# A macaron block on one core: the mixer's loop written out, and the feed-forward stages on six PSUM banks instead of eight

## The chip, the cores and the metric

The kernel runs on one core of one Trainium2 chip. The metric is device time in microseconds (us) of one execution of the whole program; three executions gave 3285.9, 3286.45 and 3291.64 us, median 3286.45. Engines are named as in the profile: PE (TensorE matmul), PEld (its weight loads), DVE (VectorE), ACT (ScalarE), POOL (GpSimd), SP (the engine that issues most transfers). Differences below 0.2% (6.6 us) are taken as no change.

## The reference

The input is 8 sequences of 1024 tokens with 256 channels, fp32. Three stages follow each other:

```python
x = x + 0.5 * ffn(layernorm(x), w_gate, w_up, w_down)
x = x + mixer(layernorm(x), ...)            # Mamba-like selective scan
x = x + 0.5 * ffn(layernorm(x), w_gate, w_up, w_down)

def ffn(x, ...):                            # every linear layer on fp4-rounded operands
    gate = fp4_linear(x, w_gate)            # 256 -> 704
    y = fp4_linear(x, w_up)                 # 256 -> 704
    return fp4_linear(silu(gate) * y, w_down)   # 704 -> 256

def mixer(h, ...):                          # 256 -> 2 x 512, conv over 4 tokens, silu
    x, z = split(h @ in_proj_w)
    x = silu(causal_conv(x))
    dt_r, B, C = split(x @ x_proj_w)        # 64, 16, 16 columns
    delta = softplus(dt_r @ dt_proj_w + b)
    # for each of 512 channels and 16 states, over 1024 tokens:
    #   s = exp(delta * A) * s + delta * B * x ;  y = sum over states of C * s
    return ((y + x * D) * silu(z)) @ out_proj_w
```

`fp4_linear` rounds both operands in blocks of 16 to a grid of 4-bit values before multiplying in fp32.

## The kernel before

**Stages.** The program runs `ffn` (with the preparation of the weights in front), `mixer`, `ffn`. Each of the three is a block of its own; all engines meet between blocks. Results between the stages lie in DRAM.

**Feed-forward.** `ffn` works on T = 32 tiles of 256 tokens, as two halves t = 0, 1 of 128 tokens. It is software-pipelined by hand: in step j each engine works on tiles j+4 to j-4 at once. The order on each engine is written in its `step` function; semaphore counts order the engines against each other. `span` (L22) writes the first eight steps and the last out as straight code and puts 16 steps, as two rounds of eight, into a hardware loop (`Fori`). PE in one step, before: `gate_up(0)` first part, `turn_h(0)`, `gate_up(0)` second part, `down(0)`, `gate_up(1)` first part, `turn_h(1)`, `gate_up(1)` second part, `turn_x`, `down(1)`. Here `gate_up` (L700) multiplies 256 channels by 1408 columns into `psG` (three banks), `turn_h` (L718) transposes the 704 hidden channels of tile j-2 into `psH` (two banks, 768 of 1024 columns used), `turn_x` (L727) transposes the quantised input of tile j+1 into `psX` (one bank), and `down` (L735) multiplies by the down weights into `psD`, one bank for each half. That makes eight banks. ACT copies `psH` to `hT` (L637, L638) and `psX` to `xT` (L677); DVE reads `psD` in `result` (L488). Semaphores `hT_kept`, `xT_kept`, `y_done` and `x_turned` tell that these were done.

**Mixer.** It runs round by round, one batch a round (`program(r, R, full)`), for r = -1 to 8: round r scans batch r and prepares parts of batches r+1 and r-1. A round has 64 slots; in each, DVE does one multiplication (L1129) and one scan (L1117) over 1024 tokens for 128 pairs of channel and state, POOL one multiplication (L962), ACT one exponential (L1063), and PE the replication of `du` (L1230), part of the sum over states (L1212), and the small jobs of a table (`JOBS`: projections, convolution, output) through two banks. The function `rounds` (L855) sets which rounds are straight code: r = -1, 0, then a hardware loop that runs three times over two rounds (r = 1 to 6), then r = 7, 8. In the loop, semaphore targets and addresses come from registers.

## Time and profile before

| what | value |
|---|---|
| median of three executions | 3286.45 us |
| profiled execution | 3285.56 us, of it span 3283.5 us |
| first feed-forward stage with preparation | to about 645 us of the span |
| mixer, from first to last scan | 751.5 to 2657 us |
| second feed-forward stage | from about 2690 us to the end |
| PE, DVE, POOL, ACT busy over the span | 83%, 81%, 66%, 52% |
| mean granted PE clock | 0.889 of full speed |

The time outside the span is 3285.56 - 3283.5 = 2.1 us. A share of the whole span is a mean over three stages with different limits, so the stages are read one by one, by stretches of the timeline. PE's records overlap their neighbours a little, so that a PE that is 50.00 of 50 us busy is one that never waits, not one at its peak.

### The profile page before, as it was taken

Reading aid. Unit: us, or ns where it says so; the run is one execution under the profiler, and the core shown is the slowest. Engines: PE = TensorE matmul, PEld = TensorE weight load, DVE = VectorE, ACT = ScalarE, POOL = GpSimd, SP = SyncE. Lnnn points to the kernel's source line nnn. Section 1 sums busy time; section 2 is a strip of 40 time slices with the busy share of each in tenths; the row PEclk is TensorE's granted clock in tenths of the full one; section 3 lists DMA queues with packets and bytes.
Section 4 is the critical chain, followed back from the end, with each engine's and each line's share of the span. In section 5 each row is a group of like instructions: output and inputs, shape, how many; then the busy total and the mean of one; then the engine's idle time right before and its main releaser. Section 6 shows DMA issues by size and latency. Waiting matters only on the chain. (4 is left out here: it accounts for less than half of the span.)

```text
span 3283.5 us, 33864 instructions
## 1 busy us (share of the span) xinstructions
PE 2736.3 (83%) x10349; PEld 1403.1 (43%) x10349; DVE 2652.0 (81%) x2498; ACT 1695.5 (52%) x2363; POOL 2174.0 (66%) x1219
## 2 busy tenths in 40 slices
PE   3999999776878978868878868978867659999998
PEld 1565656453324424414414414424412125555565
DVE  6777777408999999989999989999999946777774
ACT  3444444335756656656665655666654513444442
POOL 4566665306887877767778777777787735555552
PEclk9999999887978979969978968979966679999999
DMA  3011111108687676776777766776767720111000
GB/s 102 20 49 42 46 48 39 51 11 204 145 192 177 165 190 171 172 186 158 175 186 175 181 163 171 180 180 167 183 170 184 187 78 13 33 33 32 26 26 20
DMA packets 173331, 388.08 MB, mean 118 GB/s; under 512 B 22502, under 2 KB 90150, under 8 KB 172902
## 3 DMA queue, kind: packets, MB, share of 16 engines
q1 hardware_dynamic: 155382, 367.06, 45.0%
q10 hardware_dynamic: 17776, 18.94, 1.9%
q8 instruction: 81, 1.33, 0.2%
q14 instruction: 92, 0.75, 0.1%
HBM read 308.26 MB, written 52.49 MB: 110 GB/s over the span
## 5 line engine op out<-in xcount | busy, mean ns | idle before, releaser
L962 POOL TENSOR_TENSOR mix_scan<-mix_scan,mix_bc 128x1024 f32<-128x1024 f32 x512 | 1204.5, 2355 | 423.0 <-DVE mix_scan L1117 422.7
L1117 DVE TENSOR_TENSOR_SCAN mix_scan<-mix_decay,mix_ps_du 128x1024 f32<-128x1024 f32 x512 | 1170.0, 2285 | 72.8 <-ACT mix_decay L1063 23.5
L1129 DVE TENSOR_TENSOR mix_ps_du<-mix_ps_du,mix_bc 128x1024 f32<-128x1024 f32 x512 | 618.5, 1208 | 148.2 <-PE mix_ps_du L1230 142.3
L1230 PE MATMUL mix_ps_du<-mix_stack,mix_sel 96*128 96x512 bf16 x1024 | 367.9, 447 | 394.2 <-DVE mix_scan L1117 360.9
L711 PE MATMUL ffn_ps_gate_up<-ffn_w_gate_up,ffn_xT 128*128 128x512 f32 (+1 forms) x1536 | 662.3, 568 | 14.6 <-DVE ffn_h L479 13.0
L1063 ACT ACTIVATE mix_decay<-mix_decay,mix_a_neg 128x1024 f32<-128x1024 f32 x512 | 573.5, 1141 | 116.1 <-DMA mix_decay<-delta_rows 115.2
L741 PE MATMUL ffn_ps_down<-ffn_w_down,ffn_hT 128*128 128x256 f32 (+1 forms) x1536 | 386.4, 394 | 12.4 <-ACT ffn_hT L638 12.4
L711 PEld LDWEIGHTS ffn_ps_gate_up<-ffn_w_gate_up,ffn_xT 128*128 128x128 f32 x1536 | 273.4, 191 | 281.4 <-issue 231.2
L1230 PEld LDWEIGHTS mix_ps_du<-mix_stack,mix_sel 96*128 96x128 bf16 x1024 | 78.9, 103 | 707.3 <-DVE mix_scan L1117 581.6
L1212 PE MATMUL mix_ps_y<-mix_scan,mix_red 128*32 128x512 f32 x2048 | 342.1, 750 | 5.4 <-POOL mix_scan L962 5.4
L479 DVE TENSOR_TENSOR ffn_h<-ffn_silu_gate,ffn_ps_gate_up 128x704 f32<-128x704 f32 x128 | 113.6, 887 | 279.1 <-ACT ffn_silu_gate L643 279.1
L611 POOL TENSOR_TENSOR ffn_h_scaled<-ffn_h,ffn_h_recip 128x1408 f32<-128x1408 f32 x64 | 188.4, 2944 | 225.2 <-ACT ffn_h_recip L683 225.2
L741 PEld LDWEIGHTS ffn_ps_down<-ffn_w_down,ffn_hT 128*128 128x128 f32 (+1 forms) x1536 | 276.2, 191 | 107.7 <-issue 56.5
L637 ACT ACTIVATE ffn_hT<-ffn_ps_turned 128x640 f32<-128x640 f32 x128 | 89.9, 703 | 316.0 <-PE ffn_ps_turned L723 316.0
L1169 PE MATMUL mix_ps_job<-mix_xin,mix_conv_diag 128*128 128x256 f32 x1024 | 247.6, 386 | 2.3 <-ACT mix_xin L1015 2.3
L1169 PEld LDWEIGHTS mix_ps_job<-mix_xin,mix_conv_diag 128*128 128x128 f32 x1024 | 191.3, 191 | 86.7 <-issue 50.4
L605 POOL TENSOR_TENSOR ffn_hq<-ffn_h_scaled,ffn_h_scale 128x1408 f32<-128x1408 f32 x64 | 165.7, 2590 | 70.1 <-DVE ffn_h_scaled L534 65.9
L1021 ACT ACTIVATE mix_u<-mix_ps_job,mix_conv_b 128x256 f32<-128x256 f32 x128 | 60.2, 470 | 223.7 <-PE mix_ps_job L1169 223.7
L591 POOL TENSOR_TENSOR ffn_mv<-ffn_mv,ffn_eps 128x2 f32<-128x2 f32 x64 | 33.0, 516 | 210.0 <-DVE ffn_mv L516 205.5
L1190 PE MATMUL mix_ps_job<-mix_hnT,mix_w_in 128*128 128x512 f32 x256 | 157.1, 746 | 8.0 <-ACT mix_hnT L1000 6.6
L1162 PE MATMUL mix_ps_job<-mix_hnT,mix_w_in 128*128 128x256 f32 x512 | 145.8, 437 | 5.3 <-ACT mix_hnT L1000 5.3
L969 POOL TENSOR_TENSOR mix_delta<-mix_delta,mix_delta_u 128x1024 f32<-128x1024 f32 x32 | 75.4, 2355 | 105.8 <-ACT mix_delta_u L1080 105.8
(133 smaller groups left out, 3638.5 us busy)
## 6 DMA issues: line engine op xcount, KB each, us to landing
mix_decay<-delta_rows SPq DMA_DIRECT2D x512, 512.0 KB, 6.8
mix_stack<-mix_parts SPq DMA_DIRECT2D x384, 64.0 KB, 2.0
delta_rows<-mix_delta SPq DMA_DIRECT2D x32, 512.0 KB, 3.1
ffn_x<-_attn_hidden_states_dram SPq DMA_DIRECT2D x32, 256.0 KB, 2.9
after_ffn<-ffn_y SPq DMA_DIRECT2D x32, 256.0 KB, 3.0
normed_ffn<-ffn_y_normed SPq DMA_DIRECT2D x32, 256.0 KB, 3.0
mix_x_tokens<-normed_ffn SPq DMA_DIRECT2D x32, 256.0 KB, 11.8
mix_x_residual<-after_ffn ACTq DMA_DIRECT2D x32, 256.0 KB, 2.9
```

The lines of the kernel that those rows point to most:

```text
L605: G.tensor_tensor(blocks(hq[:, l2, :]), blocks(hn[:, l2, :]), spread(hs[:, (j - 1) % 4, :]), ALU.mult).then_inc(sig.hq_done, 1)
L611: G.tensor_tensor(blocks(hn[:, j % 2, :]), blocks(h[:, j % 2, :]), spread(hr[:, :]), ALU.mult).then_inc(sig.hn_done, 1)
L711: ins = M(psG[:, lo:hi], xT[:, j % 2, (t * KX + k) * P:(t * KX + k + 1) * P], wgu[:, k, lo:hi], start=(k == 0), stop=(k == KX - 1))
L741: ins = M(psD[:, t, 0:D], hT[0:c, t, k * P:(k + 1) * P], wd[0:c, k, :], start=(k == 0), stop=(k == KH - 1))
L962: G.tensor_tensor(wt, wt, bc[:, r % 2, 1, :], ALU.mult).then_inc(hc_done, 1)
L1063: A.activation(da[:, at % SPREADS, :], da[:, at % SPREADS, :], ACT.Exp, scale=const.aneg[:, qi:qi + 1]).then_inc(exp_done, 1)
L1117: V.tensor_tensor_scan(w[:, slot % RING, :], da[:, slot % SPREADS, :], ps_du[:, slot % 2, :], 0.0, ALU.mult, ALU.add).then_inc(scan_done, 1)
L1129: V.tensor_tensor(ps_du[:, slot % 2, :], ps_du[:, slot % 2, :], bc[:, r % 2, 0, :], ALU.mult)\
L1169: ins = M(job[:, 0:QT], const.conv_diag[:, c, t, :], xin[:, c, t:t + QT], start=(t == 0), stop=(t == TAPS - 1))
L1190: ins = M(job, const.w_in[:, k, DI + c * P:DI + (c + 1) * P], hnT[:, par, k, h * 512:(h + 1) * 512], start=(k == 0), stop=(k == KD - 1))
L1212: ins = M(y[32 * q:32 * q + 32, :], const.red[:, i, :, :].rearrange("p a b -> p (a b)"), w[:, (4 * m + q) % RING, h * 512:(h + 1) * 512], ...
L1230: ins = M(ps_du[:, slot % 2, h * 512:(h + 1) * 512], const.sel[0:SEL, i, :], stack[:, c % 2, q, h * 512:(h + 1) * 512], start=True, stop=True)
```

## The change

There are two parts. In the mixer, `rounds` writes all ten rounds out as straight code. In the feed-forward, `psX` and the second bank of `psD` go: `psD` and the first half of the transposed x share one bank, and the second half of x takes the spare columns of `psH`. `turn_x` is split into `turn_x(0)`, now ahead of `turn_h(1)`, and `turn_x(1)`, now behind `down(1)`; ACT's copy is split into two copies `keep_x(0)` (ahead of `keep_h(1)`) and `keep_x(1)` (behind `silu(1)`). Since an engine must not read a bank while PE writes into it, waits are added: `down(0)` waits for `result(1)` of the step before, `turn_x(0)` and `down(1)` for `result(0)`, `down(1)` for `keep_x(0)`, `turn_h(0)` for `keep_x(1)`. The two banks that come free are not used by anything else.

```diff
-    psH = ps_turned[:, :, :].rearrange("p a b -> p (a b)")
-    psX = a.ps("x_turned", [P, 512])
-    psD = a.ps("down", [P, 2, 512])
+    psT = ps_turned[:, :, :].rearrange("p a b -> p (a b)")
+    psDX = a.ps("down", [P, 2, D])
+    psH, psD = psT[:, 0:KH * P], psDX[:, 0, :]
+    psX = [psDX[:, 1, :], psT[:, KH * P:KH * P + D]]
...
+        def keep_x(t, j, i):
+            act.wait_ge(sig.x_turned, i * 2 + (t + 3))
+            if t == 0 and on(j, i, -1):
+                act.wait_ge(sig.gate_up_done, i * 2)
+            A.activation(xT[:, (j + 1) % 2, t * D:(t + 1) * D], psX[t], ACT.Copy).then_inc(sig.xT_kept, 1)
...
-                if t == 0:
-                    pe.wait_ge(sig.xT_kept, i + 1)
+                pe.wait_ge(sig.xT_kept, i * 2 + (t + 1))
...
+            if t == 0 and on(j, i, 0):
+                pe.wait_ge(sig.xT_kept, i * 2 + 2)
...
-        def turn_x(j, i):
-            pe.wait_ge(sig.xq_done, i + 2)
-            if on(j, i, 0):
-                pe.wait_ge(sig.xT_kept, i + 1)
-            for n in range(2 * KX):
-                ins = nc.tensor.transpose(psX[:, n * P:(n + 1) * P], xq[:, (j + 1) % 2, n * P:(n + 1) * P], ident[:, :])
+        def turn_x(t, j, i):
+            if t == 0:
+                pe.wait_ge(sig.xq_done, i + 2)
+                if on(j, i, -2):
+                    pe.wait_ge(sig.y_done, i * 2 - 3)
+            elif on(j, i, -2):
+                pe.wait_ge(sig.hT_kept, i * 2 - 2)
+            for k in range(KX):
+                n = t * KX + k
+                ins = nc.tensor.transpose(psX[t][:, k * P:(k + 1) * P], xq[:, (j + 1) % 2, n * P:(n + 1) * P],
+                                          ident[:, :])
...
-            if on(j, i, -3):
-                pe.wait_ge(sig.y_done, i * 2 + (t - 5))
+            if on(j, i, -3) or (t == 1 and on(j, i, -2)):
+                pe.wait_ge(sig.y_done, i * 2 + (t - 4))
+            if t == 1 and on(j, i, 1):
+                pe.wait_ge(sig.xT_kept, i * 2 + 3)
...
-            pairs = (B - 2) // 2
-            for r in range(-1, 1):
-                program(r, r, False)
-            if pairs > 0:
-                with eng.Fori(0, pairs) as it:
-                    for k in range(2):
-                        program(1 + k, it * 2 + (1 + k), True)
-            for r in range(1 + 2 * pairs, B + 1):
+            for r in range(-1, B + 1):
                 program(r, r, False)
```

In PE's order, one step of the feed-forward loop stands before as follows (`ffn_ps_down` is `psD`, `ffn_ps_turned` is `psH`; a wait on a row with REGISTER_ALU stands ahead of that register operation):

```order
L711 MATMUL ffn_ps_gate_up<-ffn_w_gate_up,ffn_xT 128x384 x2
L736 REGISTER_ALU
L738 REGISTER_ALU [waits ffn_hT_kept]
L741 MATMUL ffn_ps_down<-ffn_w_down,ffn_hT 128x256 [waits ffn_y_done]
...
L711 MATMUL ffn_ps_gate_up<-ffn_w_gate_up,ffn_xT 128x384 x2
L728 REGISTER_ALU
L732 MATMUL ffn_ps_x_turned<-ident,ffn_xq 128x128 [waits ffn_xT_kept,ffn_xq_done]
L732 MATMUL ffn_ps_x_turned<-ident,ffn_xq 128x128 x3
L736 REGISTER_ALU
L741 MATMUL ffn_ps_down<-ffn_w_down,ffn_hT 128x256 [waits ffn_y_done,ffn_hT_kept]
L741 MATMUL ffn_ps_down<-ffn_w_down,ffn_hT 128x256 x5
```

And the same step now:

```order
L748 REGISTER_ALU
L755 MATMUL ffn_ps_down<-ffn_w_down,ffn_hT 128x256 [waits ffn_y_done,ffn_hT_kept]
...
L743 MATMUL ffn_ps_down<-ident,ffn_xq 128x128 [waits ffn_y_done,ffn_xq_done]
...
L716 MATMUL ffn_ps_gate_up<-ffn_w_gate_up,ffn_xT 128x384 x2
L748 REGISTER_ALU
L752 REGISTER_ALU [waits ffn_y_done,ffn_hT_kept]
L755 MATMUL ffn_ps_down<-ffn_w_down,ffn_hT 128x256 [waits ffn_xT_kept]
L755 MATMUL ffn_ps_down<-ffn_w_down,ffn_hT 128x256 x5
L743 MATMUL ffn_ps_turned<-ident,ffn_xq 128x128 [waits ffn_hT_kept]
```

The first matmul of `down(0)` no longer has a register operation between its wait for `hT_kept` and itself; that of `down(1)` now has one, and it follows `gate_up(1)` directly, with no transposes of x between.

On DVE at the end of a round in the mixer (the scans stand under the name SCALAR_TENSOR_TENSOR), before (the end of the loop's body, and then what follows it):

```order
L1126 REGISTER_ALU
L1129 TENSOR_TENSOR mix_ps_du<-mix_ps_du,mix_bc 128x1024 [waits mix_rep_du]
L1117 SCALAR_TENSOR_TENSOR mix_scan<-mix_decay,mix_ps_du 128x1024 [waits mix_y_made,mix_dbu_done,mix_exp_done]
L862 REGISTER_ALU
L862 COMPARE_AND_BRANCH
L1129 TENSOR_TENSOR mix_ps_du<-mix_ps_du,mix_bc 128x1024 [waits mix_taken_B,mix_rep_du]
```

And the end of the same round now:

```order
L1138 TENSOR_TENSOR mix_ps_du<-mix_ps_du,mix_bc 128x1024 [waits mix_rep_du]
L1126 SCALAR_TENSOR_TENSOR mix_scan<-mix_decay,mix_ps_du 128x1024 [waits mix_y_made,mix_dbu_done,mix_exp_done]
L1138 TENSOR_TENSOR mix_ps_du<-mix_ps_du,mix_bc 128x1024 [waits mix_rep_du]
L1126 SCALAR_TENSOR_TENSOR mix_scan<-mix_decay,mix_ps_du 128x1024 [waits mix_y_made,mix_dbu_done,mix_exp_done]
L1138 TENSOR_TENSOR mix_ps_du<-mix_ps_du,mix_bc 128x1024 [waits mix_taken_B,mix_rep_du]
L1126 SCALAR_TENSOR_TENSOR mix_scan<-mix_decay,mix_ps_du 128x1024 [waits mix_y_made,mix_dbu_done,mix_exp_done]
```

The branch and the register operations of the loop are gone from DVE's list; the multiplications and scans stand as they did.

## Rows read from the trace of the kernel before

**Rows 1.** Page, part 2: busy tenths in 40 slices.

```profile
PE   3999999776878978868878868978867659999998
DVE  6777777408999999989999989999999946777774
```

**Rows 2.** Stretches: start:end, length, busy (x) PE PEld DVE ACT POOL, PEclk, DMA, GB/s.

```profile
300.00:350.00 50.00, 50.00 (x189) 30.17 (x188) 37.39 (x68) 23.91 (x45) 33.05 (x31) 1.00 0.15 48
```

**Rows 3.** Stretches between first scans: round 0; rounds 1-6; round 2; round 3.

```profile
751.46:984.16 232.70, 176.68 (x676) 74.04 (x675) 221.67 (x131) 148.00 (x172) 184.12 (x80) 0.84 0.76 182
984.16:2428.03 1443.87, 1181.45 (x4657) 542.95 (x4656) 1339.15 (x792) 895.10 (x1050) 1111.23 (x481) 0.85 0.72 175
1224.39:1469.77 245.38, 198.11 (x779) 90.78 (x778) 223.33 (x132) 149.26 (x176) 186.32 (x81) 0.85 0.73 178
1469.77:1705.55 235.78, 193.60 (x775) 89.39 (x774) 222.91 (x132) 149.03 (x175) 184.13 (x80) 0.86 0.71 172
```

**Rows 4.** Timeline, the loop's two jumps back: start, us, instruction, [idle before <-releaser].

```profile
1460.00 2.29 DVE L1117 TENSOR_TENSOR_SCAN mix_scan<-mix_decay,mix_ps_du 128x1024 f32<-128x1024 f32 x1
1465.59 1.89 PE L1230 MATMUL mix_ps_du<-mix_stack,mix_sel 96*128 96x512 bf16 x4 [6.03 <-issue]
1468.34 1.23 DVE L1129 TENSOR_TENSOR mix_ps_du<-mix_ps_du,mix_bc 128x1024 f32<-128x1024 f32 x1 [6.06 <-PE mix_ps_du L1230]
...
1949.33 1.23 DVE L1129 TENSOR_TENSOR mix_ps_du<-mix_ps_du,mix_bc 128x1024 f32<-128x1024 f32 x1 [5.79 <-issue]
```

**Rows 5.** DMA queues in 1460 to 1470 us: kind, packets, MB, share.

```profile
q14 instruction: 4, 0.03, 1.3%
```

**Rows 6.** DVE's waits in rounds 1 to 6: us, times, longest.

```profile
DVE mix_ps_du L1129 <- PE mix_ps_du L1230: 33.7, 24, 6.1
DVE mix_scan L1117 <- DVE mix_ps_du L1129: 11.6, 61, 0.2
DVE mix_scan L1117 <- issue: 2.7, 6, 0.5
```

**Rows 7.** Timeline of DVE in straight code, round 0.

```profile
783.05 2.29 DVE L1117 TENSOR_TENSOR_SCAN mix_scan<-mix_decay,mix_ps_du 128x1024 f32<-128x1024 f32 x1
785.26 1.21 DVE L1129 TENSOR_TENSOR mix_ps_du<-mix_ps_du,mix_bc 128x1024 f32<-128x1024 f32 x1
786.55 2.29 DVE L1117 TENSOR_TENSOR_SCAN mix_scan<-mix_decay,mix_ps_du 128x1024 f32<-128x1024 f32 x1
```

**Rows 8.** Stretches ahead of slot 51, rounds 2 and 3.

```profile
1408.00:1414.00 6.00, 6.00 (x14) 1.14 (x13) 5.76 (x5) 4.50 (x6) 3.84 (x2) 0.50 1.07 232
1651.00:1657.00 6.00, 5.34 (x20) 1.58 (x20) 5.82 (x4) 5.09 (x7) 4.38 (x2) 1.00 1.03 245
```

**Rows 9.** Timeline, single matmuls on PE in the first feed-forward stage.

```profile
306.19 0.70 PE L711 MATMUL ffn_ps_gate_up<-ffn_w_gate_up,ffn_xT 128*128 128x512 f32 x1
307.58 0.59 PE L711 MATMUL ffn_ps_gate_up<-ffn_w_gate_up,ffn_xT 128*128 128x512 f32 x1
311.68 0.45 PE L741 MATMUL ffn_ps_down<-ffn_w_down,ffn_hT 128*128 128x256 f32 x1
612.55 0.38 PE L741 MATMUL ffn_ps_down<-ffn_w_down,ffn_hT 128*128 128x256 f32 x1
615.43 0.33 PE L723 MATMUL ffn_ps_turned<-ident,ffn_hq 128*128 128x128 f32 x1
```

**Rows 10.** Timeline of one feed-forward step, 301 to 319 us.

```profile
301.86 0.70 ACT L637 ACTIVATE ffn_hT<-ffn_ps_turned 128x640 f32<-128x640 f32 x1 [4.22 <-PE ffn_ps_turned L723]
302.87 0.60 PE L732 MATMUL ffn_ps_x_turned<-ident,ffn_xq 128*128 128x128 f32 x4
303.73 0.59 ACT L677 ACTIVATE ffn_xT<-ffn_ps_x_turned 128x512 f32<-128x512 f32 x1
316.32 0.41 DVE L488 SCALAR_TENSOR_TENSOR ffn_y<-ffn_ps_down,ffn_x 128x256 f32<-128x256 f32 x1
318.16 0.82 PE L723 MATMUL ffn_ps_turned<-ident,ffn_hq 128*128 128x128 f32 x6
```

More of the change, by code:

```diff
@@ L487, in result @@
                     dve.wait_ge(sig.yn_done, i - 5)
-            V.scalar_tensor_tensor(y[:, (j - 2) % 4, t, :], psD[:, t, 0:D], 0.5, x[:, (j - 2) % 8, t, :],
+            V.scalar_tensor_tensor(y[:, (j - 2) % 4, t, :], psD, 0.5, x[:, (j - 2) % 8, t, :],
                                    ALU.mult, ALU.add).then_inc(sig.y_done, 1)
@@ L523, in step @@
                 if on(j, i, -1):
-                    dve.wait_ge(sig.x_turned, i)
+                    dve.wait_ge(sig.x_turned, i * 2)
                 V.tensor_tensor(blocks(xq[:, (j + 1) % 2, :]), blocks(xt[:, :]), spread(xs[:, (j + 1) % 2, :]),
@@ L668, in step @@
                 ins.then_inc(sig.xn_done, 1)
+            if on(j, i, 1):
+                keep_x(0, j, i)
             if on(j, i, -2):
@@ L673, in step @@
             if on(j, i, 1):
-                act.wait_ge(sig.x_turned, i + 2)
-                if on(j, i, -1):
-                    act.wait_ge(sig.gate_up_done, i * 2)
-                A.activation(xT[:, (j + 1) % 2, :], psX[:, :], ACT.Copy).then_inc(sig.xT_kept, 1)
+                keep_x(1, j, i)
             if on(j, i, 2):
@@ L736, in down @@
             pe.wait_ge(sig.hT_kept, i * 2 + (t - 3))
-            if on(j, i, -3):
-                pe.wait_ge(sig.y_done, i * 2 + (t - 5))
+            if on(j, i, -3) or (t == 1 and on(j, i, -2)):
+                pe.wait_ge(sig.y_done, i * 2 + (t - 4))
+            if t == 1 and on(j, i, 1):
+                pe.wait_ge(sig.xT_kept, i * 2 + 3)
             for k in range(KH):
                 c = min(P, F - k * P)
-                ins = M(psD[:, t, 0:D], hT[0:c, t, k * P:(k + 1) * P], wd[0:c, k, :],
+                ins = M(psD, hT[0:c, t, k * P:(k + 1) * P], wd[0:c, k, :],
                         start=(k == 0), stop=(k == KH - 1))
@@ L748, in step @@
                     gate_up(t, j, i, 0)
+                if t == 1 and on(j, i, 1):
+                    turn_x(0, j, i)
                 if on(j, i, -2):
@@ L752, in step @@
                     gate_up(t, j, i, 1)
-                if t == 1 and on(j, i, 1):
-                    turn_x(j, i)
                 if on(j, i, -2):
                     down(t, j, i)
+                if t == 1 and on(j, i, 1):
+                    turn_x(1, j, i)
         span(pe, step, -1, T + 2, 8, base)
```

## The prediction

> **What bounds the kernel now.** I read the busy tenths first, to cut the span into stages, and find three [rows 1]: slices 2 to 8 and 34 to 39, where PE stands at 9, and the long middle, where DVE does. A stretch of the feed-forward then shows PE busy 50.00 of 50 us, with DVE at 37.39 and ACT at 23.91 [rows 2]. So in the feed-forward every nanosecond that is added to PE's queue counts, and one added elsewhere counts only once it makes PE wait. In the mixer the stretches from a round's first scan to the next one's show DVE busy 221.67 of 232.70 us in round 0, and 1339.15 of 1443.87 us in the six rounds of the loop [rows 3]. DVE's idle time is what can be won there: 11.0 us in round 0, 104.7 us in rounds 1 to 6, thus 17.5 us for each. Scans follow each other at 3.50 us in straight code (783.05 to 786.55), which is 2.29 + 1.21, so nothing but idle time can go [rows 7].
>
> **The mixer's loop, the jump back.** A loop that runs three times jumps back twice. At the first jump the scan starts at 1460.00 and ends at 1462.29, and the next multiplication starts at 1468.34: DVE is idle for 6.06 us. PE, which is to give it the replicated row, itself sat for 6.03 us for nothing that the profile shows ("issue"), and DVE's second jump costs 5.79 us [rows 4]. In those 10 us the queue that carries instructions moved four packets of 8 KB (0.03 MB) [rows 5]. Round 2, which ends in such a jump, takes 245.38 us, and round 3, which does not, 235.78 [rows 3]. I take the jump as a refetch of code, all engines at once. Straight code has no jump, and rounds 0 and 7 run as straight code already. Gain 6.06 + 5.79 = 11.9 us, all on the engine that bounds the stage.
> What the Trainium skill says of it goes both ways. "Advanced Engine Details and Errata", section "Control Flow Timing", gives about 108 ns for a compare-and-branch; by that alone the two jumps would be worth 0.2 us, and I would have 11.7 us less to promise. "Runtime: NRT & Kernel Launch", section "Instruction fetch mechanics", says that a taken branch whose target lies outside the fetched window stalls for a transfer. The trace agrees with the second: 6.06 us.
>
> **The mixer's loop, register operations.** Inside the loop, 61 scans start late by 11.6 us in all behind the multiplication, 0.19 us each, and 6 more by 2.7 us for "issue" [rows 6]. In straight code the gap between multiplication and scan is 786.55 - 785.26 - 1.21 = 0.08 us [rows 7]. What goes with the registers is 11.6 - 61 x 0.08 = 6.7 us and 2.7 - 6 x 0.08 = 2.2 us, 8.9 us together. Bounds: nothing, if the gap has another cause than the register operation ahead of it, and 104.7 - 6 x 11.0 - 11.9 = 26.8 us, if the six rounds came to idle as little as round 0. The upper end is too high, since round 0 has no output jobs of an earlier batch. I take the 8.9 that has rows of its own.
> What stays: DVE's other waits for the replicated row, 33.7 - 11.9 = 21.8 us over six rounds [rows 6]. Part of them hangs on PE's clock. Ahead of slot 51 the granted clock is 0.50 in round 2 (1.2 GHz) and 1.00 in round 3 (2.4 GHz) [rows 8], and in the first DVE then waits some 2 us. Rounds begin some 6 us earlier from round 3 on, so such moments fall elsewhere: I keep the sum and put 5 us to either side. Mixer: -11.9 - 8.9 = -20.8 us.
>
> **The feed-forward, PE's own time.** The number of matmuls and transposes does not change; their neighbours do.
> First, `down` ends on a tile of 64 rows, and the weight load behind it is not hidden: the first matmul of `gate_up` lasts 0.70 us instead of 0.59. Transposes behind `down` occur in the drain of the stage, where the first lasts 0.33 us [rows 9], against 0.27 for an undisturbed one: six last 0.82 and four 0.60, so 0.11 for each start, and 0.60 - 3 x 0.11 = 0.27 [rows 10]. With `turn_x(1)` behind `down(1)`, 0.11 us is replaced by 0.06: -0.05 us in each of 29 steps that have both, in two stages, -2.9 us.
> Second, the first matmul of `down(0)` lasts 0.45 us in the loop and 0.38 outside [rows 9]: there a register operation stands between its wait for `hT_kept` and itself. By the new order `down(0)` loses this operation and `down(1)` gains it, and loses the cover of the transposes of x (0.44 us from start to start, 302.87 to 303.31). I count +0.07 and -0.07 for the 16 loop steps; if only one of the two happened, it would be 16 x 2 x 0.07 = 2.2 us to either side.
> Third, in the first two steps of each stage PE waits for the chain of silu and product, and `turn_x` lay in that wait. Now `turn_x(0)` stands in the chain, two transposes of 0.11 us in 2 steps of 2 stages: +0.9 us.
> Feed-forward: -2.9 + 0 + 0.9 = -2.0 us.
>
> **The feed-forward, the new waits.** Each was placed on the step from 301 to 319 us [rows 10].
> `turn_x(0)` waits for `result(0)`: that ends at 316.32 + 0.41 = 316.73, and the transposes would start where `turn_h(1)` does now, at 318.16. Slack 1.4 us; queued behind are `turn_h(1)`, `gate_up(1)` and with them silu and DVE.
> `down(1)` waits for the same and for `keep_x(0)`. ACT copies 640 columns in 0.70 and 512 in 0.59 us, hence 256 in about 0.37. It is idle for 4.22 us before `keep_h(1)`, and the copy runs while PE does the six transposes of `turn_h(1)`, 0.65 us. ACT is free again some 0.3 us before `keep_h(1)` may start. This is the narrowest place: `hT_kept` has no slack towards `down(1)`.
> `turn_h(0)` waits for `keep_x(1)`, which follows `down(1)` by 0.22 us of transposes and 0.4 us of copying, and has the 3.4 us of `gate_up(0)` to do it. `down(0)` waits for `result(1)` of the step before, whose bank is free some 3 us ahead.
> Behind `keep_x(1)` on ACT stand the small rescalings of the reciprocals, which wait for DVE until about then. Cost of all these waits: nothing, by these slacks; if one fails, it is paid 58 times.
>
> **The sum.** 3285.56 us of the profiled execution (3283.5 of span and 2.1 around it) - 20.8 - 2.0 = 3262.8. The median stands 0.9 us above the profiled execution, so 3263.7, rounded 3264 us, 0.7% less.
>
> **Rivals.**
> (a) Only the jumps go. The gaps of 0.19 us stay or come back as waits for PE at its lower clock, and the feed-forward gives nothing: 3286.5 - 11.9 = 3274.5 us, up to 3279 with 5 us of clock against it. For it: DVE still has 21.8 us of waits for PE that an earlier DVE only lengthens. Against it: DVE, not PE, ends nearly every slot. 0.15.
> (b) No change. The straight code has to be fetched as well, and a fetch under a loaded DMA (0.71 to 0.76 busy, rows 3) stalls the sequencers as often as the jump did: 3283 us. Against it: round 0 is straight code, under the same load, with the least idle time. Under this I also count the 0.1 us jump, whose sum is 3286.5 - 0.2 - 8.9 - 2.0 = 3275 us, with 0.01 of the chance. 0.07.
> (c) Slower. `keep_x(0)` reaches ACT late, so `keep_h(1)` starts after it and PE waits in front of `down(1)` in every step. From 22.8 / 58 = 0.4 us of wait in each step the gain is gone. If ACT gets to `keep_x(0)` only where it now gets to L637 (301.86), the wait is 0.37 us plus two hand-overs of about 0.1, 0.6 us: 58 x 0.6 = 35 us, 3263.7 + 35 = 3299 us. For it: no slack at this place, and PE bound. Against it: the 4.22 us of idle time of ACT. 0.08.
> (d) More than forecast, the loop's rounds coming near to round 0's idle time: 26.8 us in place of 8.9 at most, half of it -9 us, 3255 us. 0.08.
>
> **How the numbers follow.** The forecast has 0.62, with a range of its own from 3257 to 3271 (clock 5 us, feed-forward 2.2 us). The range for 8 in 10 takes in (d) and most of (a): 3255 to 3280 us; (c) and half of (b) lie outside. A measurement of this kernel tells 0.2% (6.6 us) from no change. Faster by more: the forecast, (a), (d) and the 0.01 of (b), together 0.85 (0.62 + 0.15 + 0.08), less 0.02 for clocks against (a), 0.83. Within 0.2%: (b) and this remainder, 0.08. Slower: (c) and a weaker form of it, 0.09.
>
> **What the profile after would show.** No idle time of 6 us on DVE between the last scan of rounds 2 and 4 and the next multiplication, and both rounds near 239 us. The group of waits of DVE's scan for its own multiplication gone from DVE's list. In the feed-forward PE still at 50.00 of 50 us, the first matmul of `gate_up(0)` at 0.59 us, and the transposes behind `down(1)` starting with 0.33. The forecast is wrong if rounds 1 to 6 take more than 1443.87 - 15 us together, if a step of the feed-forward gets longer than now by 0.1 us or more, or if PE's waits name `psX`'s new readers, L488 or ACT's copy of x.

## The result, and the profile after

The changed kernel takes 3249.02 us in the median (3248.44 to 3251.86, 4 runs), against 3287.19 us (3285.9 to 3291.64, 4 runs) of the kernel before in the same measurement: ratio 0.9883, 95% interval 0.9866 to 0.99. That is 38 us less, where 23 were forecast, and lies outside the range of 3255 to 3280. The sign and both mechanisms of the forecast hold; a third one, PE's clock, which it had set down as "5 us to either side", makes up most of the difference.

Two words are used throughout. A slot is measured on DVE, from the start of one scan to the start of the next; 3.5 us is a slot without a stall. Silu is ACT's silu in the feed-forward; there are two in each step, and a step's length is from one to the next but one. Every row and every slot length is from one profiled execution of its kernel, and executions of one kernel differ by several microseconds, so where that execution lies far from the median the text says so.

The page, part 2, shows the same three stages as in [rows 1]:

```profile
PE   2999999776878878978978978878867659999998
DVE  6777777407999999999999999999999946777775
```

From stage to stage, by the start of the first and last silu and scan in both traces:

| stretch | before | after | difference |
|---|---|---|---|
| start to first scan (feed-forward 1) | 751.5 | 750.4 | -1.1 |
| round 0 | 232.7 | 232.7 | 0.0 |
| rounds 1 to 6 | 1443.9 | 1414.0 | -29.9 |
| round 7, to its last scan | 227.1 | 227.5 | +0.4 |
| last scan to first silu of feed-forward 2 | 59.8 | 58.8 | -1.0 |
| from its first to its last silu | 536.5 | 535.5 | -1.0 |
| from there to the end | 32.0 | 27.6 | -4.4 |

The stretches of the mixer, which answer to [rows 3] (columns as in [rows 2]): rounds 1 to 6, and round 3. In the first DVE is busy almost as long as before (1337.64 against 1339.15 us), so 28.3 of the 29.9 us were its idle time.

```profile
983.17:2397.19 1414.02, 1170.33 (x4657) 540.01 (x4656) 1337.64 (x793) 894.38 (x1050) 1111.44 (x481) 0.86 0.73 179
1451.50:1687.30 235.80, 194.27 (x777) 89.59 (x776) 222.86 (x132) 149.10 (x175) 185.19 (x81) 0.86 0.74 179
```

At the place of the first jump [rows 4], DVE's timeline now has one scan 3.50 us after the other, with nothing idle between:

```profile
1447.96 2.29 DVE L1126 TENSOR_TENSOR_SCAN mix_scan<-mix_decay,mix_ps_du 128x1024 f32<-128x1024 f32 x1
1450.17 1.21 DVE L1138 TENSOR_TENSOR mix_ps_du<-mix_ps_du,mix_bc 128x1024 f32<-128x1024 f32 x1
1451.46 2.29 DVE L1126 TENSOR_TENSOR_SCAN mix_scan<-mix_decay,mix_ps_du 128x1024 f32<-128x1024 f32 x1
```

Of DVE's waits in rounds 1 to 6 (us, times, longest) the group of the scan behind its own multiplication, 61 times in [rows 6], is gone. The wait for the replicated row fell by 8.4 us from the 33.7 of [rows 6]. 6.1 of them are the first jump. The second, 5.8 us, was a group of its own in the kernel before; its row comes first, those of the changed kernel behind it:

```profile
DVE mix_ps_du L1129 <- issue: 5.8, 1, 5.8
```
```profile
DVE mix_ps_du L1138 <- PE mix_ps_du L1239: 25.3, 18, 2.6
DVE mix_scan L1126 <- ACT mix_decay L1072: 15.5, 17, 1.6
DVE mix_u L1147 <- PE mix_ps_y L1225: 3.2, 6, 0.8
DVE mix_scan L1126 <- issue: 0.9, 2, 0.5
```

The lengths of the slots, summed over rounds 1 to 6, say where the 29.9 us are: slot 63 (jumps) -12.6, slot 51 -9.4, slot 35 -2.3, slot 15 +3.2, the other 60 slots -8.7, of which 8.0 went in the gap between multiplication and scan. Slot 51 lasts 7.5 to 7.7 us in rounds 1, 2, 4 and 5 before and 4.5 in the other two; now it is long in round 5 alone. Slots 48 to 50 show how, in round 4 and in round 5 (here and below the last three columns are granted clock, DMA, GB/s):

```profile
1865.74:1876.24 10.50, 9.91 (x31) 2.98 (x30) 10.23 (x7) 7.72 (x12) 7.06 (x4) 1.00 1.04 231
2101.54:2112.37 10.83, 10.70 (x27) 3.22 (x25) 10.36 (x6) 7.21 (x10) 7.12 (x4) 0.66 0.98 223
```

The work is the same, the clock 1.00 and 0.66: the replicated row for slot 51 comes in time in the one and late in the other. In round 5 PE had been thinly busy ahead of this, 6.18 of 10.50 us in slots 44 to 46; in slot 47 it is at 0.50, the lower of its two levels (1.2 GHz). But PE was as thinly busy in round 4, 6.18 us in the same three slots, and its clock fell there too, to 0.68 in slot 47 (the first row below); it was back at 1.00 in slot 48. So a lower clock follows the thin work in both rounds, and what differs is how low it goes and how long it stays. Slot 15 is long (7.3 us) in all six rounds now, where it was 6.2 to 7.4 before, with the same pattern; PE is busy 3.38 of 7.00 us in slots 12 and 13, and in slots 14 and 15 the clock is 0.64:

```profile
1862.24:1865.74 3.50, 3.50 (x15) 1.44 (x15) 3.41 (x3) 0.55 (x1) 2.36 (x2) 0.68 1.02 226
...
2087.54:2098.04 10.50, 6.18 (x32) 2.86 (x34) 10.23 (x6) 7.28 (x9) 7.08 (x4) 0.93 1.03 237
2098.04:2101.54 3.50, 3.50 (x12) 1.32 (x13) 3.41 (x2) 0.56 (x1) 2.35 (x2) 0.50 1.05 240
...
1730.29:1737.29 7.00, 3.38 (x18) 1.64 (x20) 6.82 (x4) 5.47 (x8) 4.70 (x3) 0.82 1.02 237
1737.29:1748.12 10.83, 10.83 (x37) 5.02 (x30) 6.93 (x4) 5.36 (x7) 5.90 (x3) 0.64 1.04 242
```

In the feed-forward PE is still busy 50.00 of 50 us, as in [rows 2]. The first matmul of `gate_up(0)` now lasts 0.59 us and the transposes behind `down(1)` start with 0.33, as forecast from [rows 9]:

```profile
300.00:350.00 50.00, 50.00 (x189) 29.97 (x188) 37.63 (x71) 24.41 (x48) 33.01 (x32) 1.00 0.15 48
```
```profile
305.38 0.33 PE L743 MATMUL ffn_ps_turned<-ident,ffn_xq 128*128 128x128 f32 x1
...
305.65 0.59 PE L716 MATMUL ffn_ps_gate_up<-ffn_w_gate_up,ffn_xT 128*128 128x512 f32 x1
```

### The profile page after: what moved, and what is told of

Read it like the earlier page. It is cut to its first block and busy times, and to the rows that moved or that the text cites. A ratio compares the mean times of both kernels' runs of the same rounds, so it can differ in the third digit from the quotient of the medians.

```text
span 3246.6 us, 31734 instructions
## 1 busy us (share of the span) xinstructions
PE 2717.0 (84%) x10349; PEld 1394.6 (43%) x10349; DVE 2650.3 (82%) x2498; ACT 1705.8 (53%) x2427; POOL 2175.2 (67%) x1219
## 5 line engine op out<-in xcount | busy, mean ns | idle before, releaser
L646 ACT ACTIVATE ffn_xT<-ffn_ps_down 128x256 f32<-128x256 f32 x64 | 24.6, 384 | 230.4 <-PE ffn_ps_down L743 230.4
```

## The experiments

Medians of the kernel before, on the same chip as each group of runs: 3285.31 us for the first four, 3283.83 for the next four, 3284.19, 3285.38 and 3285.53 for those after. A "long slot 51" is one of 7.3 us or more. Two theories stood against each other throughout: REGISTERS, that register operations and jumps make the stalls by themselves, and CLOCK, that they only move a round against the moments at which PE runs at half its clock.

**One part at a time.** `e1_unroll_only` has only the mixer's part of the diff, `e2_ffn_only` only the feed-forward's.

> Only the mixer's rounds are written out; the feed-forward is that of the kernel before. Both theories give 3287 less 30 (rounds 1 to 6 were 29.9 us shorter together in the changed kernel): 3255 to 3260 us, if the mixer's part does all of it by itself. Theory CLOCK (of the 29.9 us, 21 are the jumps and the register gaps on DVE; 9 are stalls of 3 us ahead of slot 51 that fall away in three of four rounds because PE's clock happens to be high there): the number of rounds with a 7.5 us slot 51 may differ from the changed kernel's one, so 3255 to 3267. Theory REGISTERS (the 9 us are register operations on PE and ACT ahead of slot 51): at most one such round, 3255 to 3260.

> Only the feed-forward's part (six banks, x in halves); the mixer keeps its loop. From the trace of the changed kernel a step takes 17.19 us in place of 17.24 in the loop and 17.12 in place of 17.16 outside, 1.0 to 1.4 us a stage, so 3284 to 3285 us from the terms alone. CLOCK: a shift of the mixer by about 1 us may move the stalls ahead of slot 51 too, so up to 6 us to either side, and the number of 7.5 us slots 51 (4 in the kernel before) changes. REGISTERS: still 4 such slots, 3284 to 3285 us.

Measured: 3255.26 us (3253.6 to 3262.22; ratio 0.9899 to 0.993) and 3283.04 (3279.4 to 3286.37, 11 runs; 0.9982 to 1.0). The straight code gives 30 of the 38 us, and rounds 1 to 6 take 1414.0 us in it, as in the changed kernel. The feed-forward alone gives 2.3 us, and its interval reaches up to no change; that the steps are shorter is read from the traces further down. e2 has four long slots 51 like the kernel before, but in rounds 1, 2, 3 and 6 and not in 1, 2, 4 and 5.

**Jump against register operations.** `e3_one_pass` puts rounds 1 to 6 into a loop of one pass, `e4_one_jump` rounds 1 to 4 into a loop of two, `e5_regs_no_jump` rounds 1 to 5 into a loop with a step of 2 that is entered once; `e6_hint` is the kernel before with a prefetch hint for the loop's head.

```diff
# e3
+            with eng.Fori(0, 1) as it:
+                for k in range(6):
+                    program(1 + k, it * 6 + (1 + k), True)
# e4
+            with eng.Fori(0, 2) as it:
+                for k in range(2):
+                    program(1 + k, it * 2 + (1 + k), True)
# e5
+            with eng.Fori(0, 2, 2) as it:
+                for k in range(5):
+                    program(1 + k, it + (1 + k), True)
# e6
-                with eng.Fori(0, pairs) as it:
+                with eng.bass.Fori(0, pairs, engines=bass.OrderedEngineSet([eng.engine]), hint_back_edge=True) as it:
```

> The kernel before, but the loop runs once over six rounds: every wait still takes its target from a register, and no jump back is taken. If a jump costs 6 us and nothing else changes: 3287 - 12 = 3275 us, and the 0.19 us gaps between multiplication and scan are still there. REGISTERS: the stalls ahead of slot 51 stay in all or most of rounds 1 to 6, 3275 to 3280 us. CLOCK: the stalls may fall to one or two rounds with all register operations in place, then 3266 to 3272 us.

> The kernel before, but the loop runs twice over rounds 1 to 4, and rounds 5 and 6 are straight code. One jump of 6 us is left, 6 us fall away, and a third of the 9 us of register gaps: 3287 - 6 - 3 = 3278 us. The jump stands between rounds 2 and 3 with DVE idle for about 6 us; none between 4 and 5. REGISTERS: slot 51 stalls in rounds 1, 2 and perhaps 4, never in 5 and 6. CLOCK: no such pattern, total 3272 to 3281 us.

> The kernel before, but rounds 1 to 5 stand in a loop that runs once (it counts 0, then 2, up to 2), so that targets and addresses still come from registers and no jump back is taken; round 6 is straight. Theory CLOCK (stalls of 3 us ahead of slot 51 depend on where PE's clock falls, and not on register operations): 3285 - 12 for the jumps, the 0.19 us gaps stay in five rounds, and the stalls in slot 51 are as rare as in straight code if rounds of 235 us keep the clock's pattern: 3260 to 3266 us. Theory REGISTERS (the operations themselves bring the stalls): 4 or 5 of 5 rounds with a 7.5 us slot 51, 3270 to 3275 us.

> The kernel before with its loop of three passes, but each engine gets a prefetch hint for its jump back at the head of the loop. If the 6 us at a jump are the refetch of code (as the prediction has it), the idle time of DVE at 1462 and 1943 us shrinks from 6 us to under 1 us, total 3285 - 11 = 3274 us or less, down to 3262 if the stalls ahead of slot 51 go too. If the 6 us are something else of the loop (the register operations, the compare itself), nothing changes: 3285 us.

Measured: e3 3252.09 us (3251.32 to 3255.78), but its trace has none of the 0.19 us gaps and no 6 us of idle time: the loop of one pass had come out as straight code, so it tells nothing of register operations. Its one long slot 51 is in round 2, though, and not in round 5 as in e1 and the changed kernel. e4 3276.47 (3272.23 to 3280.61, 10 runs; the profiled one is the fastest), one jump of 6.2 us and long slots 51 in rounds 1, 2 and 3. e5 3273.67 (3272.47 to 3275.75): no jump, so the jumps are worth about 10 us, but 18 us above straight code, with 0.19 us gaps and a long slot 51 in every round from 1 to 6. e6 3268.65 (3265.27 to 3272.51): the 6 us at the jump are gone although it is taken twice, with 0.20 us left on DVE there, so they were the fetching of code:

```profile
1459.28 1.21 DVE L1129 TENSOR_TENSOR mix_ps_du<-mix_ps_du,mix_bc 128x1024 f32<-128x1024 f32 x1
1460.68 2.29 DVE L1117 TENSOR_TENSOR_SCAN mix_scan<-mix_decay,mix_ps_du 128x1024 f32<-128x1024 f32 x1 [0.20 <-DVE mix_ps_du L1129]
```

So far REGISTERS looked well: their gaps are 5 to 6 us, and the kernel pays 18 with them. But in e5 the straight round 6 had its slot 51 long too.

**Shifting straight code.** In `e7_shift1` and `e8_shift3` DVE writes a spare tile (896 columns) once, or three times, in round 1 of the changed kernel, and nothing else differs.

```diff
+                    if r == 1 and slot in (0,):        # e8: (0, 2, 4)
+                        V.memset(pause[:, :], 0.0)
```

> The changed kernel with one write of 896 columns (about 0.5 to 1 us) on DVE ahead of slot 0 of round 1, used by nothing: it shifts everything behind it. CLOCK: the pattern of granted clocks falls elsewhere, 1 to 5 of the rounds 1 to 6 have a 7.5 us slot 51, total 3250 to 3262 us. REGISTERS or a fixed structure: just the pause, 3250 us, with one such round as before.

> As the last, but with three such writes (ahead of slots 0, 2 and 4 of round 1), about 2 to 3 us. CLOCK: again another pattern, 3251 to 3263 us, and the number of 7.5 us slots 51 differs between the two shifted kernels. REGISTERS or a fixed structure: 3251 to 3252 us, one such round.

Measured: 3251.79 us (3249.66 to 3257.78) and 3257.91 (3253.1 to 3260.03). The profiled execution of e8, a typical one, has a long slot 51 in rounds 1, 2 and 5. That of e7 has them in rounds 1 and 2, but it is the slowest of four by 5 us and differs already in round 0, ahead of the added write (slot 51 lasts 6.5 us there), so its pattern can't be put down to the write. So slots 51 get long in straight code too, and in other rounds after a shift (e8) or without one (e3, e7). Over the profiled executions up to here they were long in 20 of 27 rounds with register operations and in 9 of 33 straight ones of rounds 1 to 6: a bias, no rule.

**Whose registers.** `e11_regs_pe` and `e12_regs_dve` are e5 with the register operations on one engine; all others have straight code.

```diff
+            looped = eng.engine == nc.tensor.engine     # e12: nc.vector.engine
+            for r in range(-1, 1 if looped else B + 1):
+                program(r, r, False)
+            if looped:
+                with eng.Fori(0, 2, 2) as it:
+                    for k in range(5):
+                        program(1 + k, it + (1 + k), True)
+                for r in range(6, B + 1):
+                    program(r, r, False)
```

> The kernel before with the rounds straight on every engine but PE; on PE rounds 1 to 5 keep their register operations (a loop that runs once, so without a jump). With them on all engines it was 3273.67, with them on none 3255.26. PE'S REGISTERS (they delay the replicate matmuls and with them move the clock): slot 51 long in three rounds or more, 3264 to 3270, while the 0.19 us gaps ahead of the scans are gone. DVE'S REGISTERS: 3252 to 3258, slot 51 long in one round or so.

> The same with the register operations on DVE alone. DVE'S REGISTERS (each delayed scan lengthens its slot, the round drifts to where the PE is at half clock at slot 51): the 0.19 us gaps are back (about 50, 5 us in all), slot 51 is long in three rounds or more: 3264 to 3274. PE'S REGISTERS: the gaps alone, 5 us, slot 51 long in one round or so: 3257 to 3262.

Measured: 3253.67 us (3252.45 to 3255.01), as e1, and 3271.07 (3269.34 to 3273.86), nearly all of e5. PE's register operations cost nothing here; DVE's are the ones that count, 17 us between these two kernels. DVE's waits in rounds 1 to 6, first with them on PE, then on DVE:

```profile
DVE mix_ps_du L1127 <- PE mix_ps_du L1228: 25.5, 18, 2.6
DVE mix_scan L1115 <- ACT mix_decay L1061: 15.4, 17, 1.5
DVE mix_u L1136 <- PE mix_ps_y L1214: 3.2, 6, 0.8
```
```profile
DVE mix_ps_du L1127 <- PE mix_ps_du L1228: 31.7, 25, 2.6
DVE mix_scan L1115 <- ACT mix_decay L1061: 16.4, 20, 1.7
DVE mix_scan L1115 <- DVE mix_ps_du L1127: 10.3, 52, 0.5
DVE mix_u L1136 <- PE mix_ps_y L1214: 9.3, 16, 0.9
```

Rounds 1 to 6 take 20.5 us more in e12 than in e11. The gaps are 10.3 - 52 x 0.09 = 5.6 of them; the waits for PE grew by 6.2 and 6.1 us, those for ACT by 1.0. e12 has five long slots 51, e11 one.

**Holding the clock up.** PE writes the replicated rows of some slots several times over: the same two matmuls into the same bank, ahead of the semaphore that hands it on. Nothing is left out.

```diff
+        WARM = {12: 1, 13: 2, 14: 3, 15: 1, 44: 1, 45: 2, 46: 2, 47: 3, 48: 1}    # e9 (straight), e10 (loop)
+        WARM = {12: 1, 13: 2, 14: 3, 15: 1}                                       # e13 (straight)
+        WARM = {12: 1, 13: 2, 14: 3, 15: 1, 44: 1, 45: 2, 46: 2, 47: 3,
+                48: 2, 49: 2, 50: 2, 51: 1}                                       # e14 (straight), e15 (loop), e16 (e12)
+        # e18 (straight): as e14, with 22: 2, 24: 3, 25: 3, 26: 1, 34: 2, 35: 1
-                for h in range(2):
+                for h in list(range(2)) * (1 + WARM.get(slot, 0)):
                     ins = M(ps_du[:, slot % 2, h * 512:(h + 1) * 512], const.sel[0:SEL, i, :], ...
```

> The changed kernel, in which the PE writes the replicated rows of slots 12 to 15 and 44 to 48 two to four times over (the same two matmuls again, into the same bank, before the semaphore that hands it on), so that it is not idle in the slots 11 to 14 and 43 to 47. In the changed kernel its clock stands at 0.50 in slots 14 and 15 of every round 1 to 6 (slot 15 lasts 7.3 us) and at 0.50 again in slots 48 and 50 of round 5 alone (slot 51 lasts 7.6 us). CLOCK (the long slots are the PE at half clock after slots in which it had little to do): slot 15 falls from 7.3 to about 4.5 us or less in six rounds and slot 51 of no round is long, so 3249 - 6 x 2.8 - 3 = 3229, at most 3235. WORK (the long slots are long because so much is asked of the PE there, whatever its clock): the doubled matmuls add to it, slot 15 stays at 7.3 us or more, 3250 to 3265.

> The kernel before, with the same repeated replicate matmuls (slots 12 to 15 and 44 to 48) and its loop as it is. CLOCK: slot 51 is long in no round although the register operations and both jumps are there, and slot 15 shortens in six rounds: 3284 - 4 x 3.0 - 6 x 2.8 = 3255, with the 0.19 us gaps ahead of the scans and the two 6 us jumps still in the trace. REGISTERS (register operations by themselves make slot 51 long): slot 51 stays at 7.5 us in four rounds and only slot 15 can shorten: 3267 to 3284.

Measured: 3247.76 us (3246.35 to 3248.15) and 3280.85 (3277.68 to 3288.98, 10 runs). Neither theory's number came (e10's profiled execution is the slowest of ten). Slot 15 did fall from 7.3 to 3.7 or 3.8 us in rounds 1 to 6 but for one of 4.1, as CLOCK wants. Slot 51 got longer, 9.9 us in four straight rounds and 9.7 to 10.0 in all six of the loop: the repeats stopped at slot 48, and the low clock came later, in slots 50 and 51. Round 4 of e9, slots 48 and 49, then 50 and 51:

```profile
1861.84:1868.84 7.00, 5.53 (x16) 1.65 (x20) 6.82 (x4) 6.00 (x9) 4.71 (x3) 0.89 1.03 227
```
```profile
1868.84:1882.31 13.47, 12.72 (x28) 2.80 (x22) 8.07 (x5) 7.04 (x8) 5.92 (x3) 0.55 0.70 172
```

That called for repeats up to slot 51, and for slot 15 alone:

> The changed kernel with the repeated replicate matmuls only for slots 12 to 15. Repeating them for 44 to 48 too had shortened slot 15 from 7.3 to 3.8 us and less, and lengthened slot 51 from 4.5 to 9.9 us in four rounds, with the PE at 0.50 in slots 50 and 51 instead of 46 to 48. CLOCK: slot 15 short in every round, slot 51 as in the changed kernel or in straight code at large (4.5 us, 7.5 in one or two rounds): 3249 - 6 x 3.5 + 3 = 3228 to 3234. If the shorter rounds (232 us) bring slot 51 into the low clock each time: + 6 x 3.0, 3246.

> The changed kernel with the matmuls repeated for slots 12 to 15 and for 44 to 51, so that the PE has no thin slot ahead of slot 51. CLOCK: neither slot 15 nor slot 51 is long in any round, the granted clock in slots 46 to 51 is 1.00: 3249 - 6 x 3.5 - 3 = 3225, up to 3232 where the repeated matmuls of slot 51 delay its product a little. WORK: slot 51 lasts 7.5 us or more in most rounds: 3240 to 3255.

> The kernel before (loop, register operations, both jumps) with the matmuls repeated as in the last. CLOCK: slots 15 and 51 short in every round in spite of the register operations: 3284 - 6 x 3.5 - 4 x 3.0 = 3251, and 21 us to 27 us above the straight kernel with the same repeats (two jumps 12, gaps 9, feed-forward 2 to 6): the register operations then cost no more than their gaps. REGISTERS: slot 51 long in four rounds or more, 3263 or above.

> The kernel with the register operations on DVE alone (3271.07 as it stood, 16 us above straight code), with the matmuls repeated for slots 12 to 15 and 44 to 51. CLOCK (5 us of the 16 are the 0.19 us gaps themselves, the rest is the PE's clock at slot 51 in five rounds): slots 15 and 51 short, 3271 - 6 x 3.5 - 5 x 3.0 = 3235, 4 to 8 us above the straight kernel with the same repeats, once the feed-forward change's 2 to 6 us are taken off. REGISTERS (all of the 16 are the register operations' own): 16 us above it, less the feed-forward change.

| kernel | median us (lowest to highest) | ratio, 95% | rounds 1 to 6 | long slots 51 |
|---|---|---|---|---|
| e13, straight, slots 12 to 15 | 3222.47 (3220.86 to 3225.03) | 0.9792 to 0.9825 | 1390.0 | 1 |
| e14, straight, both | 3219.72 (3218.03 to 3223.19) | 0.9783 to 0.9816 | 1386.5 | 0 |
| e15, loop, both | 3248.48 (3246.61 to 3257.52) | 0.9868 to 0.9901 | 1417.4 | 0 |
| e16, DVE's registers, both | 3233.78 (3232.47 to 3237.68) | 0.9829 to 0.9862 | 1396.8 | 0 |

e13 to e16 lie 1 to 6 us below CLOCK's numbers (3228, 3225, 3251, 3235); e13 and e14 are below its whole ranges. WORK is out, and so is REGISTERS for slot 51: with the clock held up it is long in no round, whether register operations and jumps are there or not, and 264 more matmuls in rounds 1 to 6 of e14 made them 27.5 us shorter. 21.6 of them are slot 15 and 2.9 slot 51; e13, which leaves slot 51 alone, is 3.5 us behind e14 there, mostly by its one long slot 51.

For the price of DVE's register operations neither theory was right. They cost 1434.5 - 1414.0 = 20.5 us in rounds 1 to 6 in e12 against e1, and 1396.8 - 1386.5 = 10.3 us in e16 against e14. By the medians e16 is 14 us above e14, 12 without the feed-forward's 2, where CLOCK had 4 to 8 and REGISTERS 16. So half of the price went when the clock was held up, and what is left is more than the bare gaps. The rows of e14 are slots 14 and 15, slots 48 to 50, and rounds 1 to 6; below them slots 48 to 50 of e15:

```profile
1723.28:1730.52 7.24, 7.24 (x37) 3.72 (x30) 6.83 (x5) 6.54 (x8) 4.96 (x3) 1.00 1.03 227
1848.21:1858.71 10.50, 10.50 (x36) 3.55 (x35) 10.23 (x7) 7.02 (x11) 7.07 (x4) 1.00 1.02 234
982.90:2369.40 1386.50, 1181.89 (x4921) 554.96 (x4920) 1336.60 (x792) 893.74 (x1050) 1111.46 (x481) 0.90 0.75 182
```
```profile
1870.82:1881.33 10.51, 10.51 (x37) 3.45 (x34) 10.24 (x7) 7.03 (x11) 6.98 (x4) 1.00 1.04 234
```

In e14 the same two slots 14 and 15 take 7.24 us at 1.00 in place of 10.83 at 0.64.

CLOCK put the loop e15 at 21 to 27 us above e14; by the medians it is 28.8. e15's profiled execution is the slowest of four, by 9 us, and so shows more than that: rounds 1 to 6 take 30.9 us longer than in e14. There slot 35 lasts 6.5 us in rounds 2, 4 and 6, where nothing is repeated; it was 6.6 in round 6 of the kernel before. The rows are slots 34 and 35 of e15, in round 3 and in round 4; the longer one has the lower clock:

```profile
1584.02:1587.52 3.50, 3.50 (x13) 1.30 (x6) 3.41 (x3) 0.00 (x0) 2.36 (x2) 0.58 0.64 157
1587.52:1592.65 5.13, 5.13 (x26) 2.97 (x25) 4.55 (x3) 3.70 (x4) 3.58 (x2) 1.00 0.00 0
...
1817.21:1820.71 3.50, 3.50 (x10) 0.85 (x4) 3.41 (x3) 0.00 (x0) 2.35 (x2) 0.50 0.88 201
1820.71:1827.26 6.55, 6.55 (x28) 4.05 (x27) 4.66 (x4) 3.70 (x4) 3.57 (x2) 0.86 0.01 2
```

**The feed-forward's order.** `e17_turn_first` is the changed kernel with `turn_x(1)` ahead of `down(1)`; `e18_warm_more` repeats still more rows.

```diff
+                if t == 1 and on(j, i, 1):
+                    turn_x(1, j, i)
                 if on(j, i, -2):
                     down(t, j, i)
-                if t == 1 and on(j, i, 1):
-                    turn_x(1, j, i)
```

> The changed kernel with the second half of x transposed ahead of down(1) instead of behind it, as the whole was before; everything else (two halves, banks given up) stays. ORDER (the 0.05 us a step come from the transposes standing behind the 64-row tile of down, so that gate_up's first matmul no longer does): a step in the loop goes back from 17.19 to 17.24 us, and a stage of 31 steps from 535.5 to about 537 us between its first and last silu. OTHER (the gain is the shared bank's or the split's): 17.19 and 535.5 stay. In the median about 3 us at most: 3249 to 3252.

> The changed kernel with the replicate matmuls repeated also for slots 22 to 26 and 34, 35, ahead of the places at which slots 28, 35 and 39 are some 0.5 to 1 us longer than 3.5 us in rounds 3 to 6; without these repeats it was 3219.72. CLOCK (these too follow a PE at 0.50 in slots 24 to 26 and 34): up to 2.3 us in each of four rounds, 3211 to 3217. WORK (too much is asked of the PE there): no change or longer, 3219 to 3226.

Measured: e17 3249.6 us (3248.48 to 3250.38), no difference that the medians can tell. Its trace can: steps outside the loop are back at 17.16 us (17.12 in the changed kernel), and the first matmul of `gate_up(0)` is back at 0.70. Inside the loop the step is 17.17 instead of the 17.24 that I expected: `down(0)` has no register operation of its own here, and that of `down(1)` stands behind transposes again, so both start with 0.38 us and neither shows the 0.07.

```profile
305.13 0.38 PE L755 MATMUL ffn_ps_down<-ffn_w_down,ffn_hT 64*128 64x256 f32 x1
305.44 0.70 PE L716 MATMUL ffn_ps_gate_up<-ffn_w_gate_up,ffn_xT 128*128 128x512 f32 x1
```

e18: 3217.63 us (3212.67 to 3218.29; ratio 0.9775 to 0.9808). It is the fastest of all, but its runs overlap with e14's, and the median lies between CLOCK's range and WORK's, so it decides nothing. Its profiled execution is the fastest of four, by 5 us: rounds 1 to 6 take 1381.7 us, 4.8 less than in e14; slot 28 is no longer long, and slot 3 has become so (5.8 us) in rounds 3 and 5.

## Why the prediction was off

**The jumps: right.** -11.9 forecast; slot 63 gave 12.6, and e6 shows that it was a fetch of code. Of the two statements of the Trainium skill that the prediction weighed, "Runtime: NRT & Kernel Launch" on instruction fetch agrees with the traces and the 108 ns of "Advanced Engine Details and Errata" for a branch does not cover it: 6.06 us in the loop as written.

**The register operations: right in the size of their own row.** -8.9 forecast; the gap ahead of the scans gave 8.0 in the 60 slots other than 15, 35, 51 and 63. As a price of register operations the term is too small: with the clock held up, e16 lies 10.3 us above e14 in rounds 1 to 6, for five rounds with DVE's alone. e15's profiled execution is 30.9 above e14 there, 12.7 of it in slot 63, so 18 us with registers on all engines. 5.9 of that stand in slot 35, at a clock of 0.50 and 0.86 around it in round 4; I did not hold the clock up there in the loop, so that it is the clock is read from the rows, not tested.

**PE's clock: the step that failed.** The prediction read the mechanism right from [rows 8], and then wrote "such moments fall elsewhere: I keep the sum and put 5 us to either side". That step set the clock's part of the sum at nothing. The moments were not equally likely on both sides, as rows of the kernel before could have told. A long slot 51 costs 3.0 us, four of six rounds had one, and the rounds that are straight code in the kernel before, 0 and 7, had none. The forecast's "both rounds near 239 us" for rounds 2 and 4 is their 245 us less the jump, with the long slot 51 left in; they took 235.5 and 235.3. Its working for this step had a slip as well: "33.7 - 11.9 = 21.8" takes both jumps off a group that holds only the first, so 27.6 us of waits for PE's row were left, not 21.8, and slot 15, 6.2 to 7.4 us in every one of the six rounds, was not looked at. What the term measured: slot 51 -9.4, slot 35 -2.3, slot 15 +3.2, together -8.5 us in the mixer, and another -4.4 at the very end, a drain that the prediction did not place on the clock at all. The rows, before and after, from 3.5 us behind the last silu on:

```profile
3254.90:3283.40 28.50, 19.19 (x67) 12.92 (x66) 5.94 (x9) 4.97 (x10) 5.17 (x2) 0.82 0.08 28
```
```profile
3222.40:3246.50 24.10, 14.83 (x68) 10.27 (x66) 5.99 (x9) 4.97 (x10) 5.17 (x2) 1.00 0.09 33
```

From the last silu to the end it is 27.6 us in eleven of the twenty traces, all at a granted clock of 1.00, 29.2 to 29.4 in seven at 0.94, and 30.4 (e2) and 32.0 (before) at 0.83 and 0.84. Both forms of the feed-forward occur among the shortest, so the 4.4 us are not the change's doing. No run held the clock up there, and what makes this end long or short stays open. A sum by the rows would have been 20.8 + 2.0 + 12.9 = 35.7, against 36.9 us of span. That the clock made slots 15 and 51 long is shown (e13 to e16). Why register operations of DVE make a long slot 51 more frequent stays open: with them and without jumps a round lasts 238 to 240 us (e5, e12), without them mostly 233 to 236, but 3 us of that are the long slot itself.

**The feed-forward: right.** -2.0 forecast, -2.0 found: -1.0 us between first and last silu in each stage. The -1.0 us between the last scan and the second stage's first silu is not counted: that stretch scatters from 58.6 to 61.8 us over all kernels, with both forms of the feed-forward. The weight load behind the 64-row tile gave 17.24 to 17.19 in the loop and 17.16 to 17.12 outside, the term of 0.05; e17 takes it back outside the loop. The two 0.07 us of register operations cancelled, as forecast. The slower fill was +0.29 us in the first step and nothing in the second: +0.6 for both stages, not +0.9.

**The new waits: right.** ACT copies 256 columns in 0.38 us (0.37 estimated) and then waits 0.35 us for `turn_h(1)`, so rival (c) had 0.35 us to spare and did not happen; PE waits for nothing from 120 to 600 us:

```profile
317.87 0.38 ACT L646 ACTIVATE ffn_xT<-ffn_ps_down 128x256 f32<-128x256 f32 x1 [3.64 <-PE ffn_ps_down L743]
318.61 0.70 ACT L638 ACTIVATE ffn_hT<-ffn_ps_turned 128x640 f32<-128x640 f32 x1 [0.35 <-PE ffn_ps_turned L730]
```

**The rivals.** (a) and (b) are out: gaps and jumps went, and straight code is fetched without a stall. (d), with 0.08, came nearest: rounds 1 to 6 now idle 10.0 to 16.1 us each, round 0 10.9. It put 9 us beyond the sum, and 9.1 came there (29.9 against 20.8); its 3255 us misses the drain. It named a size and no cause, so that the size fits is luck.

## What to carry to other kernels

A jump back in a long loop can stall the engine that bounds the stage (here 6 us each time); a prefetch hint or straight code removed it here, and straight code also removed the register operations ahead of the waits of the engine that bounds the stage.

Where an engine has two clocks, a stall that appears in some rounds and not in others is a term of the sum and not a symmetric error: count how many rounds have it, price it, and ask whether the rounds that already look like the new code have it.

Useless work on an engine that is not the bound can be the cheapest fix: repeating some matmuls ahead of slot 15 alone brought 3249 to 3222 us. The repeats have to reach up to the place where PE is needed quickly: stopped three slots short of slot 51, they moved the low clock onto it and gave nearly all of the gain back (3248).

## What the runs showed of the hardware that I had not expected

- A register operation on PE's queue cost nothing (e11), on DVE's 17 us over five rounds (e12 against e11), of which 5.6 us were its own gaps.
- More matmuls took less time: rounds 1 to 6 with 4921 of them recorded take 1386.5 us at a mean granted clock of 0.90, with 4657 of them 1414.0 us at 0.86.
- Three short writes of DVE in round 1, some 2.4 us in all, raised the median by 9 us, to 3257.91 (e8), with long slots 51 in rounds 1, 2 and 5 in place of 5 alone.
- The end of the last stage, with the same code, took 27.6 us at a granted clock of 1.00 (e16) and 32.0 at 0.84 (the kernel before).
